# A fused group-norm, gate and 3x3-convolution kernel: the convolution moved to eight array tiles, with column folds, a channel norm on ScalarE, a new order of VectorE and POOL, and six x slots

## The chip, the cores and the metric

The kernel runs on one core of one Trainium2 chip. The metric is the device time of one execution in microseconds (us). Three runs of the kernel before took 4295.59, 4297.46 and 4298.4 us: the median is 4297.46 us. TensorE is called PE, its weight loads PEld, VectorE DVE, ScalarE ACT, GpSimd POOL, and SyncE, which issues all the DMAs, SP.

## The reference

The input x is (8, 512, 128, 128) in fp32. It is first group-normalised over 32 groups of 16 channels, and each of the 8*32 = 256 groups is then an image gx of 16 channels and 128x128 pixels:

```python
gap = mean(gx, (2, 3)); gmp = max(gx, (2, 3))
ch = conv1x1(concat([gap, gmp], 1), w_cc, b_cc)
channel_weight = sigmoid(_gn(ch, gn1_w, gn1_b))      # _gn: one element for each channel
hw = conv1x1(concat([mean over w, mean over h]), w_s1, b_s1)
pos_h = sigmoid(conv1x1(xh, w_ph, b_ph)); pos_w = sigmoid(conv1x1(xw, w_pw, b_pw))
sx = conv3x3(gx * pos_h * pos_w, w_s3) + b_s3        # 16 -> 16 channels, padding SAME
spatial_weight = sigmoid(_gn(sx, gn2_w, gn2_b))      # over the 128x128 pixels of each channel
return x + gx * (channel_weight * spatial_weight)
```

So each group needs statistics of x (mean, variance, row sums, column sums, maxima), two position gates from them, the gated image, a 3x3 convolution of it, the statistics of that, and a last multiply-add.

## The kernel before, in words

**Layout.** A unit is two groups (j = 0, 1); there are UNITS = 128. Image row 8b + r (b = 0 to 15, r = 0 to 7) of channel c lies on partition 8c + r, in band b. So a group is a tile of 128 partitions by 16 bands by 128 pixels, 2048 elements a partition. x comes into `xt` (XS = 4 slots of one unit each), in eight DMAs of 128 KB for each group, and the result leaves from `sp_buf` in eight more (L222, L230).

**Loop.** Every engine has its own `body(t, q)`, and `turns` (L165) runs it for all t. In body t PE does the convolution of unit t; DVE, ACT and POOL prepare the gates of unit a = t + 1; DVE reduces unit c = t + 2; the result of unit b = t - 1 is finished; SP loads unit t + 3 into the slot of unit t - 1, after waiting for `final` of that unit (L220). The order of instructions in each body is written by hand, with semaphores between engines.

**Convolution.** `conv(h, first, last)` (L695) handles a half group, h = 0 to 3: two PSUM banks of four bands each. A 3x3 kernel reaches the rows 8b - 1 and 8b + 8, which lie in the neighbouring bands. `W_conv` (128x128 for each kw) covers what stays in the band. For the rest SP copies the edge rows of the gated image, in three shifts, into `halo` (96 partitions, L245), and one more matmul with `W_halo` adds them. So each bank takes 3 + 1 matmuls of 512 columns, a unit 8 banks and thus 32 matmuls. Between them PE does small matmuls that sum over partitions: `mean`, `maxima`, `mean2`, `variance`, `var2`, `positions`, `channel` (all through `mm`, L637). Each fp32 matmul of the source is two instructions in the trace, each with a weight load of its own; this document calls them passes.

**VectorE.** Body t (L529 to L618) in its order: `finish(b, 0)` (two passes over the group, L524 and L527), the small `sums_n` (L543, L545), row sums of group 0 of unit c (L554), `gmx` and `var_e`, row sums of group 1, `tot`, `gate_hr` (L594), the column sums of both groups (L560, a reduction over a rearranged view), `ch` (L603), the maxima (L607), `modulate` of both groups (L567), `finish(b, 1)`.

**ACT** evicts conv_ps, 1024 elements at a time (L370), squares x (L435) and the convolution (L390) with a sum, makes the gates (L447, L452), the affine pair `scale`, `bias` (L408, L411), the sigmoid (L416) and `cgate` (L471). **POOL** makes `gate_w * gate_hr` (L323), the powers of -0.5 (L343, L275), `kfac` (L336), and the channel branch: three small operations in `channel_in` (L284 to L289) and nine in `channel_norm` (L297 to L313), each waiting for the one before.

## Time and profile of the kernel before

| what | value |
|---|---|
| median of three runs | 4297.46 us |
| the profiled execution: its own time | 4296.2 us |
| the profiled execution: span of the trace | 4294.3 us |
| PE, DVE busy, share of the span | 94%, 94% |
| ACT, POOL busy, share of the span | 61%, 41% |
| mean granted TensorE clock | 0.965 |
| HBM read and written | 268.64 MB, 268.44 MB |

The profile page gives shares of the whole span. Since the kernel is one loop of 128 equal bodies, it is read here per unit: a group's total divided by 128, and timelines of one body. Busy times of groups overlap by up to 0.1 us at their seams, so the step from one start to the next is shorter than a mean duration. Most of the time below is told as a period, the time from one unit to the next.

### The profile page before, as it was taken

What the parts mean: (1) busy time and instruction counts of PE and PEld (TensorE: products, weight loads), DVE (VectorE), ACT (ScalarE), POOL (GpSimd) and SP (SyncE); (2) the same over time, 40 slices, a digit from 0 to 9 for tenths busy, and PEclk for the clock granted to TensorE, in tenths of its full rate; (3) what the DMA queues carried; (4) which work ended last, traced back from release to release, by engine and by line L of the source; (5) the groups of instructions that cost most, each with busy time, mean ns of one, the idle gap of its engine ahead of it and who ended that gap; (6) DMA issues with size and microseconds to landing.
All of it is one profiled execution on the core that took longest, in us unless ns stands there. A gap on an engine that the chain in (4) does not pass through costs nothing.

```text
span 4294.3 us, 55492 instructions
## 1 busy us (share of the span) xinstructions
PE 4041.4 (94%) x11016; PEld 1938.2 (45%) x11016; DVE 4018.4 (94%) x2719; ACT 2624.4 (61%) x4354; POOL 1775.4 (41%) x2314
## 2 busy tenths in 40 slices
PE   5999999999999999999999999999999999999997
PEld 2444444444444444444444444444444444444443
DVE  7999999999999999999999999999999999999996
ACT  3566566666665666666656666666666666665665
POOL 3443444444434434443344434344444344434443
PEclk9999999999999999999999999999999999999998
DMA  6777777777777777777777777777777777777775
GB/s 124 163 173 173 172 175 169 175 172 173 172 173 169 177 173 172 175 167 178 172 172 172 172 176 172 171 172 176 168 177 173 172 175 167 177 173 173 171 177 123
DMA packets 1147751, 730.57 MB, mean 170 GB/s; under 512 B 74144, under 2 KB 1122976, under 8 KB 1147552
## 3 DMA queue, kind: packets, MB, share of 16 engines
q1 hardware_dynamic: 1147552, 728.87, 74.7%
q14 instruction: 190, 1.56, 0.1%
q8 instruction: 9, 0.15, 0.0%
HBM read 268.64 MB, written 268.44 MB: 125 GB/s over the span
## 4 chain that ended last, share of the span: by engine, by line
DVE 53%; issue 18%; SPq 11%; DMA 9%; PE 6%; POOL 1%; ACT 1%; DVEq 1%; POOLq 0%; ACTq 0%
DVE sums L560 13%; DVE mx L607 12%; SPq L222 11%; DMA xt<-in_x 9%; DVE sp_buf L524 7%; DVE sums L554 7%; DVE gated L567 7%; DVE sp_buf L527 6%; PE conv_ps L637 5%; POOL rstd L275 1%; ACT sp_buf L416 1%; DVE gate_hr L594 0%; PE pos_ps L637 0%; DVE ch L603 0%; DVE sums_n L545 0%
## 5 line engine op out<-in xcount | busy, mean ns | idle before, releaser
L637 PE MATMUL conv_ps<-gated,W_conv 128*128 128x512 f32 x6144 | 2973.1, 619 | 16.5 <-DVE gated L567 16.3
L637 PEld LDWEIGHTS conv_ps<-gated,W_conv 128*128 128x128 f32 x6144 | 1143.4, 197 | 1100.0 <-issue 1071.7
L637 PE MATMUL conv_ps<-halo,W_halo 96*128 96x512 f32 x2048 | 1027.7, 604 | 2.1 <-DMA halo<-gated 1.6
L370 ACT ACTIVATE sp_buf<-conv_ps,weights 128x1024 f32<-128x1024 f32 x512 | 565.3, 1104 | 747.8 <-PE conv_ps L637 747.5
L323 POOL TENSOR_TENSOR gated<-gate_w,gate_hr 128x2048 f32<-128x2048 f32 x256 | 918.7, 3609 | 166.9 <-DVE gate_hr L594 157.6
L560 DVE TENSOR_REDUCE sums<-xt 128x128 f32<-128x2048 f32 x256 | 943.6, 3725 | 0.0
L554 DVE TENSOR_REDUCE sums<-xt 128x16 f32<-128x2048 f32 x256 | 584.2, 2282 | 171.5 <-DMA xt<-in_x 171.4
L524 DVE SCALAR_TENSOR_TENSOR sp_buf<-xt,negm,sp_buf 128x2048 f32<-128x2048 f32 x256 | 600.6, 2346 | 38.3 <-ACT sp_buf L416 38.3
L527 DVE SCALAR_TENSOR_TENSOR sp_buf<-sp_buf,kfac,xt 128x2048 f32<-128x2048 f32 x256 | 602.1, 2352 | 9.0
L567 DVE SCALAR_TENSOR_TENSOR gated<-xt,negm,gated 128x2048 f32<-128x2048 f32 x256 | 593.9, 2361 | 0.0
L343 POOL TENSOR_TENSOR rstd<-var_e,consts 128x2 f32<-128x2 f32 x128 | 89.8, 701 | 1176.8 <-DVE var_e L581 1176.8
L607 DVE TENSOR_REDUCE mx<-xt 128x2 f32<-128x4096 f32 x128 | 563.7, 4404 | 0.0
L416 ACT ACTIVATE sp_buf<-sp_buf,bias,scale 128x2048 f32<-128x2048 f32 x256 | 536.4, 2095 | 8.5
L637 PEld LDWEIGHTS conv_ps<-halo,W_halo 96*128 96x128 f32 x2048 | 367.1, 190 | 379.9 <-issue 354.8
L390 ACT ACTIVATE junk<-sp_buf,negm 128x2048 bf16<-128x2048 f32 x256 | 512.5, 2002 | 41.5 <-ACT share L384 41.0
L435 ACT ACTIVATE junk<-xt,negm 128x2048 bf16<-128x2048 f32 x256 | 510.5, 1994 | 19.0 <-ACT negm L429 11.9
L275 POOL TENSOR_TENSOR rstd<-var_e,consts 128x1 f32<-128x1 f32 x256 | 234.2, 915 | 674.7 <-ACT var_e L399 674.7
L336 POOL TENSOR_TENSOR kfac<-cgate,rstd 128x2 f32<-128x2 f32 x128 | 164.8, 1288 | 390.5 <-ACT cgate L471 390.5
L447 ACT ACTIVATE gate_h<-pos_ps,b_pos,rstd 128x16 f32<-128x16 f32 x256 | 79.0, 359 | 294.6 <-POOL rstd L343 294.6
L399 ACT ACTIVATE var_e<-gn_ps,consts 128x1 f32<-128x1 f32 x256 | 68.3, 267 | 301.0 <-PE gn_ps L637 301.0
L637 PE MATMUL pos_ps<-sums_n,W_rows 128*128 128x32 f32 x256 | 57.1, 308 | 159.0 <-DVE sums_n L545 159.0
L408 ACT ACTIVATE scale<-rstd,weights 128x1 f32<-128x1 f32 x256 | 74.0, 289 | 192.5 <-POOL rstd L275 192.5
(79 smaller groups left out, 2174.4 us busy)
## 6 DMA issues: line engine op xcount, KB each, us to landing
xt<-in_x SPq DMA_DIRECT2D x2048, 128.0 KB, 3.0
out<-sp_buf SPq DMA_DIRECT2D x2048, 128.0 KB, 2.5
halo<-gated SPq DMA_DIRECT2D x512, 365.2 KB, 6.0
weights<-in_by_channel SPq DMA_DIRECT2D x1, 116.5 KB, 2.6
S_chan<-in_same_channel SPq DMA_DIRECT2D x1, 64.0 KB, 1.9
whalo_in<-in_wconv SPq DMA_DIRECT2D x2, 3.0 KB, 1.8
masks<-in_row_masks SPq DMA_DIRECT2D x1, 12.0 KB, 1.9
hmask<-in_halo_mask SPq DMA_DIRECT2D x1, 3.0 KB, 1.9
```

What stands on the lines that cost most here:

```text
L323: nc.gpsimd.tensor_tensor(gated[:, d, j, :, 1:1 + W], gate_w[:, d, j].unsqueeze(1).to_broadcast([P, NB, W]), gate_hr[:, d, j].unsqueeze(2) ...
L370: nc.scalar.activation(sp_buf[:, g, k * 8:k * 8 + 8], conv_ps[:, h % 2], ACT.Identity, bias=V["b_s3"], accum_out=ssum2[:, g, k:k + 1]).the ...
L390: nc.scalar.activation(junk[:, 2], sp_buf[:, g].rearrange("p b w -> p (b w)"), ACT.Square, bias=negm2[:, g:g + 1], accum_out=ssq2[:, g:g + ...
L416: nc.scalar.activation(flat, flat, ACT.Sigmoid, scale=scale2[:, g:g + 1], bias=bias2[:, g:g + 1]).then_inc(sig2, 1)
L435: nc.scalar.activation(junk[:, j], xt[:, sa, j].rearrange("p b w -> p (b w)"), ACT.Square, bias=negm[:, sa, j:j + 1], accum_out=ssq[:, da, ...
L524: nc.vector.scalar_tensor_tensor(flat, xf, negm[:, s, j:j + 1], flat, ALU.add, ALU.mult).then_inc(fin_a, 1)
L527: nc.vector.scalar_tensor_tensor(flat, flat, kfac[:, s, j:j + 1], xf, ALU.mult, ALU.add).then_inc(final, 1)
L554: nc.vector.tensor_reduce(sums[:, dc, j, 0:NB], xt[:, sc, j], AX_X, ALU.add).then_inc(sums_done, 1)
L560: nc.vector.tensor_reduce(sums[:, dc, j, NB:], xt[:, sc, j].rearrange("p b w -> p w b"), AX_X, ALU.add).then_inc(sums_done, 1)
L567: nc.vector.scalar_tensor_tensor(gated[:, da, j, :, 1:1 + W], xt[:, sa, j], negm[:, sa, j:j + 1], gated[:, da, j, :, 1:1 + W], ALU.add, AL ...
L607: nc.vector.tensor_reduce(mx[:, dc], xt[:, sc].rearrange("p j b w -> p j (b w)"), AX_X, ALU.max).then_inc(mx_done, 1)
L637: return nc.tensor.matmul(ps, lhsT, rhs, start=start, stop=stop)
```

## The change

x slots XS go from 4 to 6, and the loop runs six bodies a turn. Image row 8b + r of channel c now lies on partition 32*(r//2) + 2c + r%2, so that each 32 partitions hold two rows of all channels. `gated` gets an empty band at each end (18 bands), and the halo tile, its DMAs and `W_halo` go. A convolution matmul is one tile of 64 input partitions by 32 output partitions: `tiles` issues four of them (one for each pair of output rows), `slot(n)` does bank n of the unit, for each kw the four tiles of the upper 64 partitions on bank n and the four of the lower 64 partitions on bank n - 1. The row that comes from another band is reached by a band index that is one lower or higher. conv_ps is four banks, evicted two at a time as before in size. Column sums become two elementwise folds (16 bands to 8 to 4) and four accumulating matmuls; the mean is subtracted through a further matmul (`W_cols_m`, `W_rows_m`), so `sums_n` goes. `channel_in` goes into matmuls (`W_gap_m`, `W_ch_m`), `channel_norm` goes from POOL to ACT and its power joins `rstd` on POOL, as four columns.

```diff
-XS = 4
+XS = 6
...
-        gated = sb("gated", [P, 2, 2, NB, WP])
-        halo = sb("halo", [HALO, 2, 2, NB * WP])
+        gated = sb("gated", [P, 2, 2, NB + 2, WP])
...
-        conv_ps = psum("conv_ps", [P, 2, HALF * BB, W])
+        conv_ps = psum("conv_ps", [P, BANKS, BB, W])
...
+        def row_partitions(r):
+            at = QUAD * (r // 2) + r % 2
+            return slice(at, QUAD * (r // 2 + 1), 2)
...
-                v, vs = t + 3, (q + 3) % XS
-                h, hs = t + 1, (q + 1) % 2
+                v, vs = t + XS - 1, (q + XS - 1) % XS
...
                 load(0)
                 store(0)
-                halo_rows(0)
-                halo_rows(1)
                 load(1)
                 store(1)
...
# POOL
+                if real(a):
+                    pool.wait_ge(var_done, a + 1)
+                    if real(t):
+                        pool.wait_ge(ch_var, 6 * t + 6)
...
+                    nc.gpsimd.tensor_tensor(rstd[:, sa], var_e[:, sa % 2], consts[:, 0:4],
+                                            ALU.pow).then_inc(rstd_done, 1)
...
+                if real(a):
+                    gate_products(a, sa, 0)
+                if real(b):
+                    rstd2_power(b, sb_, 1)
...
+                    nc.gpsimd.tensor_tensor(kfac[:, q], cgate[:, q % 2], rstd[:, q, 0:2],
                                             ALU.mult).then_inc(kfac_done, 1)
                 if real(a):
...
                     gate_products(a, sa, 1)
-                    channel_norm(a, sa)
                 if real(t):
                     rstd2_power(t, q, 0)
...
# ACT
+            def channel_variance(u, s):
+
+                act.wait_ge(ch_mm, u + 1)
...
+                for j in range(2):
+                    nc.scalar.activation(ch[:, 0, j:j + 1], cw_ps[:, j:j + 1], ACT.Identity,
+                                         scale=rstd[:, s, j:j + 1], bias=V["b_cc"]).then_inc(ch_var, 1)
+                for j in range(2):
+                    act.wait_ge(ch_var, 6 * u + j + 1)
+                    nc.scalar.activation(ch[:, 1, j:j + 1], ch[:, 0, j:j + 1], ACT.Identity, scale=-1.0,
+                                         bias=ch[:, 0, j:j + 1]).then_inc(ch_var, 1)
+                act.wait_ge(ch_var, 6 * u + 4)
+                nc.scalar.activation(ch[:, 2], ch[:, 1], ACT.Square).then_inc(ch_var, 1)
...
+                nc.scalar.activation(var_e[:, (s + 1) % 2, 2:4], ch[:, 2], ACT.Identity,
+                                     bias=consts[:, 4:5]).then_inc(ch_var, 1)
+
+            def channel_gate(u, s):
+
+                act.wait_ge(rstd_done, u + 2)
+                for j in range(2):
+                    nc.scalar.activation(ch[:, 3, j:j + 1], ch[:, 1, j:j + 1], ACT.Copy,
+                                         scale=rstd[:, (s + 1) % XS, 2 + j:3 + j]).then_inc(ch_norm, 1)
...
+                nc.scalar.activation(cgate[:, s % 2], ch[:, 3], ACT.Sigmoid, scale=V["gn1_w"],
+                                     bias=V["gn1_b"]).then_inc(cgate_done, 1)
...
+            def body(t, q, k):
...
+                if real(a):
+                    mean1(a, sa)
+                    square1(a, sa, 0, loads(k, q, 1))
                 if real(b):
                     evacuate(b, sb_, 3)
                 if real(a):
...
+                    square1(a, sa, 1, loads(k, q, 1))
+                    gates(a, sa)
+                if real(t):
+                    evacuate(t, q, 0)
                 if real(b):
                     square2(b, sb_, 1)
                 if real(t):
...
+                    channel_gate(t, q)
+                    evacuate(t, q, 1)
                 if real(b):
                     variance2(b, sb_, 1)
...
                     spatial_gate(b, sb_, 1)
                 if real(t):
                     square2(t, q, 0)
+                    evacuate(t, q, 2)
+                if real(a):
+                    channel_variance(a, sa)
                 if real(t):
...
                     variance2(t, q, 0)
                     spatial_gate(t, q, 0)
...
# DVE
+            def fold_columns(u, s, j, come):
...
+                nc.vector.tensor_tensor(fold8[:], xt[:, s, j, 0:8], xt[:, s, j, 8:16],
+                                        ALU.add).then_inc(fold8_done, 1)
+                dve.wait_ge(fold8_done, n + 1)
...
+                nc.vector.tensor_tensor(fold4[:, s % 2, j], fold8[:, 0:4], fold8[:, 4:8],
+                                        ALU.add).then_inc(fold4_done, 1)
...
+                if real(c):
+                    fold_columns(c, sc, 0, loads(k, q, 2))
+                    fold_columns(c, sc, 1, loads(k, q, 2))
                 if real(b):
...
+                    gate_x(b, sb_, 0)
                 if real(a):
...
+                    channel_maxima(a, sa)
+                    variance1(a, sa)
+                if real(b):
+                    add_x(b, sb_, 0)
                 if real(a):
...
+                    scaled_row_gate(a, sa)
                 if real(c):
...
+                    row_sums(c, sc, 0)
+                    row_sums(c, sc, 1)
+                    totals(c, sc)
+                    maxima(c, sc)
                 if real(a):
...
+                    modulate(a, sa, 0)
+                    modulate(a, sa, 1)
                 if real(b):
...
+                    gate_x(b, sb_, 1)
+                    add_x(b, sb_, 1)
...
# PE
+                        mm(pos[:, :, 0:NB], W_rows[:, :], sums[:, da], stop=False)
+                        mm(pos[:, :, 0:NB], W_rows_m[:, :], shift.to_broadcast([P, 2, NB]), start=False)
+                        for i in range(4):
+                            mm(pos[:, :, NB:NB + W], W_cols[:, :], fold4[:, da, :, i], start=i == 0, stop=False)
+                        mm(pos[:, :, NB:NB + W], W_cols_m[:, :], shift.to_broadcast([P, 2, W]),
+                           start=False).then_inc(pos_mm, 1)
...
+                def tiles(u, d, n, half, kw, start):
+
+                    j, k = n // BANKS, n % BANKS
+                    for o in range(PAIRS):
+                        band = 1 + BB * k
+                        if half == 1 and o == 0:
+                            band -= 1
+                        if half == 0 and o == PAIRS - 1:
+                            band += 1
+                        rows = slice(ROW_TILE * half, ROW_TILE * (half + 1))
+                        cols = slice(QUAD * o, QUAD * (o + 1))
+                        ins = mm(conv_ps[cols, k], W_conv[rows, kw, cols],
+                                 gated[rows, d, j, band:band + BB, kw:kw + W], start=start and kw == 0,
+                                 stop=not start and kw == KW - 1)
+                    return ins
+
+                def slot(n, first=0, last=KW):
...
+                        if n % 2 == 0 and later(4 * t + n // 2, 2):
+                            pe.wait_ge(evac, 4 * t + n // 2 - 1)
...
+                    for kw in range(first, last):
+                        if real(t):
+                            ins = tiles(t, q % 2, n, 0, kw, True)
...
+                            if n > 0:
+                                ins = tiles(t, q % 2, n - 1, 1, kw, False)
+                            else:
+                                ins = tiles(b, sb_ % 2, 7, 1, kw, False)
...
                 mean()
-                conv(0, 0, 2)
                 maxima()
...
+                slot(0)
+                slot(1)
                 mean2(b, sb_, 1)
...
+                positions()
+                slot(2, 0, 1)
                 variance()
...
+                slot(2, 1, KW)
+                slot(3)
+                slot(4)
                 var2(b, sb_, 1)
...
                 channel()
...
+                slot(5)
                 mean2(t, q, 0)
...
+                slot(6)
+                slot(7)
                 var2(t, q, 0)
```

In the setup, `expand` writes each 128x128 weight in four instructions of 32 columns instead of one, and `gated` is cleared whole.

## Rows read from the trace of the kernel before

**Rows 1.** The profile page, engines' busy time and chain.

```profile
PE 4041.4 (94%) x11016; PEld 1938.2 (45%) x11016; DVE 4018.4 (94%) x2719; ACT 2624.4 (61%) x4354; POOL 1775.4 (41%) x2314
...
DVE 53%; issue 18%; SPq 11%; DMA 9%; PE 6%; POOL 1%; ACT 1%; DVEq 1%; POOLq 0%; ACTq 0%
```

**Rows 2.** Source view of L587: duration min/median/max, first and last start.

```profile
L587 DVE TENSOR_REDUCE tot<-sums x128: 185/186/190, 21.1 to 4194.6; 128x2 f32<-128x32 f32 x128
```

**Rows 3.** Windows: us, busy of each engine, PEclk, DMA share.

```profile
2002.11:2032.67 30.56, 30.56 (x87) 14.58 (x86) 29.31 (x22) 20.73 (x35) 13.49 (x18) 1.00 0.72 173
500.00:4200.00 3700.00, 3533.83 (x9636) 1693.38 (x9635) 3511.69 (x2354) 2293.83 (x3811) 1550.35 (x2018) 0.96 0.76 173
```

**Rows 4.** Waits view, all engines: total us, times, longest us.

```profile
ACT gate_h L447 <- POOL rstd L343: 294.6, 112, 5.8
...
DVE sums L554 <- DMA xt<-in_x: 171.4, 115, 5.7
...
DVE sp_buf L524 <- ACT sp_buf L416: 38.3, 17, 11.5
```

**Rows 5.** Chain of waits, 2028 to 2048 us: start us, us, what.

```profile
2034.96 2.36 DVE sp_buf L527
...
2037.49 0.60 SPq L222
...
2041.93 0.54 SPq L222
...
2042.65 3.25 DMA xt<-in_x
```

**Rows 6.** Timelines of PE and PEld, 2000 to 2006 us.

```profile
2002.11 0.28 PE L637 MATMUL norm_ps<-tot,M_all 128*128 128x2 f32 x2
...
2001.68 0.19 PEld L637 LDWEIGHTS norm_ps<-tot,M_all 128*128 128x128 f32 x1 [0.24 <-issue]
2002.11 0.19 PEld L637 LDWEIGHTS norm_ps<-tot,M_all 128*128 128x128 f32 x1 [0.24 <-issue]
2002.22 0.30 PEld L637 LDWEIGHTS conv_ps<-gated,W_conv 128*128 128x128 f32 x2
```

**Rows 7.** Groups by line and shape, PE: xcount, busy us, mean ns, idle before.

```profile
L637 PE MATMUL conv_ps<-gated,W_conv 128*128 128x512 f32 x6144 | 2973.1, 619 | 16.5 <-DVE gated L567 16.3
...
L637 PE MATMUL conv_ps<-halo,W_halo 96*128 96x512 f32 x2048 | 1027.7, 604 | 2.1 <-DMA halo<-gated 1.6
```

**Rows 8.** Timeline of DVE, one body.

```profile
2004.65 2.35 DVE L524 SCALAR_TENSOR_TENSOR sp_buf<-xt,negm,sp_buf 128x2048 f32<-128x2048 f32 x1
...
2009.30 0.23 DVE L543 TENSOR_SCALAR sums_n<-sums,negm 128x16 f32<-128x16 f32 x1
...
2009.97 2.28 DVE L554 TENSOR_REDUCE sums<-xt 128x16 f32<-128x2048 f32 x1
...
2016.13 7.39 DVE L560 TENSOR_REDUCE sums<-xt 128x128 f32<-128x2048 f32 x2
...
2023.51 4.40 DVE L607 TENSOR_REDUCE mx<-xt 128x2 f32<-128x4096 f32 x1
...
2037.23 2.34 DVE L524 SCALAR_TENSOR_TENSOR sp_buf<-xt,negm,sp_buf 128x2048 f32<-128x2048 f32 x1
```

**Rows 9.** Groups by line and shape, DVE.

```profile
L524 DVE SCALAR_TENSOR_TENSOR sp_buf<-xt,negm,sp_buf 128x2048 f32<-128x2048 f32 x256 | 600.6, 2346 | 38.3 <-ACT sp_buf L416 38.3
...
L488 DVE TENSOR_TENSOR w_part<-weights,masks 128x128 f32<-128x128 f32 x6 | 1.8, 292 | 0.2
```

**Rows 10.** Groups by line and shape, ACT and POOL.

```profile
L411 ACT ACTIVATE bias<-negm,weights,scale 128x1 f32<-128x1 f32 x256 | 99.1, 387 | 8.5
...
L307 POOL TENSOR_TENSOR ch<-ch,consts 128x2 f32<-128x2 f32 x128 | 89.8, 702 | 10.0
...
L408 ACT ACTIVATE scale<-rstd,weights 128x1 f32<-128x1 f32 x256 | 74.0, 289 | 192.5 <-POOL rstd L275 192.5
...
L303 POOL TENSOR_TENSOR ch<-ch 128x2 f32<-128x2 f32 x128 | 27.0, 211 | 10.0
```

More of the change, by code:

```diff
@@ L73, in conv_attention @@
         S_chan = sb("S_chan", [P, P])
-        sums = sb("sums", [P, 2, 2, NB + W])
-        sums_n = sb("sums_n", [P, 2, 2, NB + W])
+        sums = sb("sums", [P, 2, 2, NB])
+        fold8 = sb("fold8", [P, 8, W])
+        fold4 = sb("fold4", [P, 2, 2, 4, W])
+        W_rows_m = sb("W_rows_m", [P, P])
+        W_cols_m = sb("W_cols_m", [P, P])
         tot = sb("tot", [P, 2, 2])
@@ L167, in turns, with loads @@
             first, last = 1, (UNITS - 4) // PER
-            for t in range(-3, first * PER):
-                body(t, t % PER)
+            for t in range(1 - XS, first * PER):
+                body(t, t % PER, t // PER)
             with eng.Fori(first, last) as turn:
                 for q in range(PER):
-                    body(turn * PER + q, q)
+                    body(turn * PER + q, q, turn)
             for t in range(last * PER, UNITS + 1):
-                body(t, t % PER)
+                body(t, t % PER, t // PER)
+        def loads(k, q, d):
+            return 16 * RB * (k + (q + d) // XS + 1)
         ends = [0]
@@ L417, in spatial_gate, with mean1, square1 @@
                                      bias=bias2[:, g:g + 1]).then_inc(sig2, 1)
-            def body(t, q):
+            def mean1(u, s):
+                act.wait_ge(mean_mm, u + 1)
+                if later(u, XS):
+                    act.wait_ge(final, 2 * (u - XS) + 2)
+                nc.scalar.activation(negm[:, s], norm_ps[:, 0:2], ACT.Copy, scale=-1.0).then_inc(negm_done, 1)
+            def square1(u, s, j, come):
+                if j == 0:
+                    act.wait_ge(negm_done, u + 1)
+                act.wait_ge(x_in[s][j], come)
+                if later(u, 1):
+                    act.wait_ge(sq_done, 2 * u + j - 1)
+                nc.scalar.activation(junk[:, j], xt[:, s, j].rearrange("p b w -> p (b w)"), ACT.Square,
+                                     bias=negm[:, s, j:j + 1], accum_out=ssq[:, s % 2, j:j + 1]).then_inc(sq_done, 1)
@@ L525, in finish, with add_x @@
+            def add_x(u, s, j):
+                g = 2 * (s % 2) + j
+                n = 2 * u + j
+                flat = sp_buf[:, g].rearrange("p b w -> p (b w)")
                 dve.wait_ge(fin_a, n + 1)
                 dve.wait_ge(kfac_done, u + 1)
-                nc.vector.scalar_tensor_tensor(flat, flat, kfac[:, s, j:j + 1], xf, ALU.mult, ALU.add).then_inc(final, 1)
-            def body(t, q):
+                nc.vector.scalar_tensor_tensor(flat, flat, kfac[:, s, j:j + 1],
+                                               xt[:, s, j].rearrange("p b w -> p (b w)"),
+                                               ALU.mult, ALU.add).then_inc(final, 1)
@@ new lines, in scaled_row_gate, with modulate @@
+            def scaled_row_gate(u, s):
+                dve.wait_ge(gates_done, 4 * u + 4)
+                dve.wait_ge(rstd_done, u + 1)
+                if later(u, 2):
+                    dve.wait_ge(gp_done, 2 * (u - 1))
+                nc.vector.tensor_tensor(gate_hr[:, s % 2], gate_h[:, s % 2],
+                                        rstd[:, s, 0:2].unsqueeze(2).to_broadcast([P, 2, NB]),
+                                        ALU.mult).then_inc(ghr_done, 1)
+            def modulate(u, s, j):
+                dve.wait_ge(gp_done, 2 * u + j + 1)
+                inner = gated[:, s % 2, j, 1:1 + NB, 1:1 + W]
+                nc.vector.scalar_tensor_tensor(inner, xt[:, s, j], negm[:, s, j:j + 1], inner,
+                                               ALU.add, ALU.mult).then_inc(mod_done, 1)
@@ L615, in body @@
-                modulate(0)
-                modulate(1)
+                    modulate(a, sa, 0)
+                    modulate(a, sa, 1)
                 if real(b):
-                    finish(b, sb_, 1)
+                    gate_x(b, sb_, 1)
+                    add_x(b, sb_, 1)
             turns(dve, body)
```

437 lines of the change are left out of this document (159 added, 278 removed).

## The prediction, made before the changed kernel was run

> **What bounds the kernel now.** I read the engines' busy shares first. DVE and PE both stand at 94% [rows 1], so one engine's share decides nothing. Then the rhythm: `tot` starts once a unit, first at 21.1 and last at 4194.6 us [rows 2], which makes a period of 4173.5/127 = 32.86 us. The rest of the execution (4296.2 us by its own time) is 123 us of start and end. I make the sum against that execution; it stands 1.3 us below the median of the runs, which I neglect.
>
> PE is not the bound: between two `mean` matmuls with no stall it does a whole unit in 30.56 us [rows 3], 2.3 us less than the period. The chain is 53% DVE, 18% issue gaps, 11% SP's queue, 9% DMA and 6% PE [rows 1], and in one body it shows the loop: DVE ends `final`, SP issues the eight loads into the freed slot (the first at 2037.49, the seventh at 2041.93, so 0.74 us each), the last lands 3.25 us after its issue, and only then do the row sums start [rows 5]. DVE waits for x 171.4 us in all [rows 4], 1.34 us a unit. So DVE's own work is 32.86 - 1.34 = 31.5 us a unit, with 38.3/128 = 0.3 us of waiting for ACT in it [rows 4].
>
> **VectorE.** Out go the four `sums_n` (2009.30 to 2009.97, 0.67 us) and both column sums with `ch` (2016.13 to 2023.51, 7.38 us) [rows 8]: 8.05 us. In come, for each group, an elementwise add of 1024 elements and one of 512. No such add of these lengths is in the trace. An elementwise add of 128 took 0.292 us and a two-tensor pass over 2048 took 2.346 [rows 9]; a straight line between them gives 1.25 and 0.70 us. The bounds for a unit's folds: 1.15 ns an element (2346/2048) and nothing fixed gives 3.5 us; the column sums' own 3.69 us for 2048, spent on 1536, gives 5.5. I take the line, 3.9 us, because the pass it leans on is the same kind of work. DVE then needs 31.5 - 8.05 + 3.9 = 27.4 us (27.0 to 29.0). Splitting `finish` in two moves work and adds none; between `gate_x` and `add_x` now stand two tiny operations, which cover the latency of the first.
>
> **x slots.** A load of unit t+5 still waits for `final` of unit t-1, but DVE needs it three bodies later instead of one. The whole SP and DMA piece of the chain, about 1.34 us, is thus covered by two bodies. It is already out of my 27.4. SP still issues 32 DMAs, 32*0.74 = 23.7 us, and loses the four halo ones; it fits under 27 but not far under: the next thing late there would be the stores, on which evictions wait. DMA was busy 0.76 of the time with the halo traffic [rows 3] and loses that part.
>
> **TensorE, convolution.** A pass of 512 columns steps by 0.43 us (weight loads at 2001.68 and 2002.11 [rows 6]), at a granted clock of 1.00 in this stretch and 0.96 in the loop as a whole [rows 3], that is at the 2.4 GHz level nearly all the time. Now 64 passes, 27.5 us, leaving 30.56 - 27.5 = 3.0 us for the small matmuls. After: 8 slots x 3 kw x 8 tiles = 192 matmuls, 384 passes. If the eight tiles stream at once this is 24 full matmuls: 48*0.43 = 20.6 us, or 54 ns a pass. That is the lower bound; with no overlap, the upper bound, it is 384*0.43 = 165 us. The trace has no tile, so what speaks for one end? Issue: between two weight loads of a small matmul lie 0.11 us (2002.11, 2002.22 [rows 6]) for 128 columns; a tile loads 32, a quarter, 28 ns, under the 54. So loads need not hold the tiles up, and the halves of the array differ in rows, columns and banks. I take 20.6.
>
> The TensorE page of the Trainium skill (TensorE: Matmul & The Clock Gate, "Measured speedup vs the span model") gives 10.6x for 16 tiles and 2.38x for 3 column tiles, with one pass a tile. No run here shows it.
>
> **TensorE, the rest.** `positions` gains four matmuls of 256 columns (2*0.215 = 0.43 us each, half of 512): 1.7 us. `W_rows_m` and one channel matmul are load-bound, 2*0.11 us each: 0.4. Then the changes between whole-array and tile matmuls: five stretches of small matmuls a unit, ten changes. If each waits for the matmul in flight to leave the array, it costs what a matmul lasts beyond its step, 604 [rows 7] - 430 = 174 ns: 1.7 us. The bounds are nothing and a whole matmul, 6 us. I take 1.7, as the array must be emptied but not idle longer. Sum: 20.6 + 3.0 + 1.7 + 0.4 + 1.7 = 27.5 us (25.8 to 31.8).
>
> The Trainium skill (TensorEngine Tiling (Array Packing), "Key Properties") says that changing the tiling mode drains the engine. Without it the sum would be 25.8 and DVE alone the bound.
>
> **ACT and POOL.** ACT works 2624.4/128 = 20.5 us [rows 1] and gains eight one-or-two-element operations, at 0.29 to 0.39 us [rows 10]: 2.6. It waits 294.6/128 = 2.3 us for `rstd` [rows 4]. 23.1 + 2.3 = 25.4 us: under the others, though its evictions are due sooner. A bank pair came free again after a half of 6.9 us; now one slot, 2.6 us, lies between its last write and its next, and ACT's squares and sigmoids are 2 us long. POOL loses nine and three small operations (0.70, and 0.2 each [rows 10]), about 2.9 of 13.9 us. But `gate_products(a, 1)` now stands behind `rstd2_power(b, 1)` and `kfac`, which wait for ACT; DVE's 9 us of row sums and maxima (2*2.28 + 4.40 [rows 8]) cover that; without it `modulate` would be late.
>
> **The sum.** DVE 27.4 and PE 27.5 us are level, and each waits for the other once or twice a unit. For the seams I add 0.6 us, twice what DVE waits for ACT now: 28.1 us a unit. The setup has 45 more small linked DVE instructions, under 0.29 us each [rows 9], and clears all of `gated` (9360 elements, at most 10.7 us at 1.15 ns); the first shortened units give part of this back: +7. So 127*28.1 + 123 + 7 = 3699, say **3700 us**.
>
> **The rivals.**
> First, *the tiles do not run side by side*. Each tile gets two passes in a row. If a matmul may start only after the one before it in the program, the second pass of a tile holds the queue until the first has streamed, and each tile matmul costs 0.43 us: 192*0.43 = 82.6, plus 6.9 = 89.5 us a unit, 11,500 us. For it: the two passes in sequence, each with its own load [rows 6]. Against it: nothing in this trace. The point of decision is 67.6 ns a pass ((32.86 - 6.9)/384); above it the kernel is slower. The TensorE page of the Trainium skill ("The mechanism") says that matmuls start and end strictly in program order, which would give just this. A milder form, the tiles packed at two thirds: 31.2 + 6.9 = 38.1 us, 4970 us. Chance of both: 0.18, two thirds of it for the first.
>
> Second, *PE or ACT is the bound, still faster*. At 60 ns a pass and 0.4 us a change PE needs 23.0 + 5.1 + 4 = 32.1 us: 4210 us. Or each of four evictions comes 0.5 us late for its bank and PE stands: 27.5 + 2 = 29.5 us, 3880 us. ACT's order is strict and it has 3 us to spare. 0.30.
>
> Third, *DVE alone*: no change cost, full cover: 26.8 to 27.4 us, 3530 to 3610 us. 0.10.
>
> Fourth, *no gain*: the tile passes land between 66 and 69 ns by chance. 0.02.
>
> **How the numbers follow.** My forecast, 27.5 to 29.0 us a unit (3620 to 3810 us), has 0.40. Adding the third and nearly all of the second, 3520 to 4230 us holds about 8 in 10. Faster by over 0.2% (about what a measurement of this kernel can tell from no change): 0.40 + 0.30 + 0.10 = 0.80; within: 0.02; slower: 0.18.
>
> **What would show it.** Column adds at 1.25 and 0.70 us on DVE; no wait of row sums or folds for x; tile passes stepping by about 54 ns, eight in flight; a stop of 0.17 us where small matmuls follow tiles; a step of `tot` of 28.1 us; ACT at 82% busy. The forecast falls if the tile passes step by more than 60 ns, or if PE's waits for evictions pass 1 us a unit.

## The result, and the profile after

The changed kernel takes 4532.26 us (median of four runs, 4530.24 to 4536.99) against 4296.52 us before: 1.0551 times the time before (95% interval 1.0533 to 1.057). The forecast was 3700 us. The page of the changed kernel:

```profile
span 4528.4 us, 140298 instructions
PE 3905.6 (86%) x53512; PEld 1885.3 (42%) x53512; DVE 3564.3 (79%) x2380; ACT 2889.1 (64%) x5378; POOL 1706.1 (38%) x777
```

Every engine has less to do than in [rows 1] or has room left, and none is full. The beat comes from the source view of `tot` (duration, first and last start):

```profile
L560 DVE TENSOR_REDUCE tot<-sums x128: 185/186/188, 42.2 to 4436.4; 128x2 f32<-128x32 f32 x128
```

(4436.4 - 42.2)/127 = 34.60 us a unit, where [rows 2] gave 32.86. What stands outside the 127 periods is 4532 - 4394 = 138 us; I had 123 + 7.

TensorE in one body (start us, us, then in brackets the idle time before and what ended it):

```profile
2007.90 0.38 PE L653 MATMUL gn_ps<-ssq,M_chan 128*128 128x1 f32 x2
...
2008.67 5.74 PE L653 MATMUL conv_ps<-gated,W_conv 64*32 64x512 f32 x96
2017.62 0.38 PE L653 MATMUL gn_ps<-ssum,M_chan 128*128 128x2 f32 x2 [3.20 <-ACT sp_buf L322]
...
2018.41 3.62 PE L653 MATMUL pos_ps<-fold,W_cols 128*128 128x256 f32 x8
...
2022.39 1.09 PE L653 MATMUL conv_ps<-gated,W_conv 64*32 64x512 f32 x16
2023.41 0.38 PE L653 MATMUL norm_ps<-ssq,M_all 128*128 128x2 f32 x2
2023.73 4.88 PE L653 MATMUL conv_ps<-gated,W_conv 64*32 64x512 f32 x80
2029.79 3.11 PE L653 MATMUL conv_ps<-gated,W_conv 64*32 64x512 f32 x48 [1.18 <-ACT sp_buf L322]
...
2042.54 0.38 PE L653 MATMUL gn_ps<-ssq,M_chan 128*128 128x1 f32 x2
```

Three things are to be seen. Two slots of convolution, as much work as twelve passes over the whole array (12*0.43 = 5.16 us), take 5.74 us, so the tiles do run side by side. PE stands twice for an eviction (L322 is `evacuate`), 3.20 us ahead of `mean2(b, 1)` and 1.18 us ahead of slot 4. And the eight fold passes, 256 columns each, take 3.62 us where eight halves of 0.43 us should take 1.7. The windows view of the same stretches says why (us; busy us of PE, PEld, DVE, ACT, POOL; granted clock; DMA share; GB/s):

```profile
2008.67:2014.40 5.73, 5.73 (x97) 2.39 (x96) 5.69 (x3) 2.85 (x5) 2.58 (x1) 1.00 0.01 3
...
2017.62:2022.00 4.38, 4.38 (x15) 3.73 (x16) 1.96 (x2) 1.93 (x2) 0.00 (x0) 0.61 0.66 171
```

Before the stand the clock is 1.00 (2.4 GHz); after it, most of the positions run at 1.2 GHz. Over the whole span the mean granted clock is 0.938, and 0.965 before. As the clock has two levels, one half the other, a mean m means 2(1 - m) of the span at the low one: 561 us now, 301 us before.

The timelines of ACT, POOL and DVE around these waits, one fence for each:

```profile
2011.36 0.29 ACT L360 ACTIVATE scale<-rstd,weights 128x1 f32<-128x1 f32 x1 [2.78 <-POOL rstd L260]
...
2012.11 2.10 ACT L368 ACTIVATE sp_buf<-sp_buf,bias,scale 128x2048 f32<-128x2048 f32 x1
...
2014.38 2.00 ACT L385 ACTIVATE junk<-xt,negm 128x2048 bf16<-128x2048 f32 x1
...
2016.38 1.09 ACT L322 ACTIVATE sp_buf<-conv_ps,weights 128x1024 f32<-128x1024 f32 x1
...
2027.23 0.62 ACT L395 ACTIVATE gate_h<-pos_ps,b_pos,rstd 128x16 f32<-128x16 f32 x2 [7.68 <-POOL rstd L285]
...
2028.43 1.12 ACT L322 ACTIVATE sp_buf<-conv_ps,weights 128x1024 f32<-128x1024 f32 x1
```

```profile
2008.75 2.58 POOL L260 TENSOR_TENSOR rstd<-var_e,consts 128x1 f32<-128x1 f32 x1 [4.63 <-ACT var_e L351]
2024.26 2.88 POOL L285 TENSOR_TENSOR rstd<-var_e,consts 128x4 f32<-128x4 f32 x1 [12.93 <-DVE var_e L589]
```

```profile
2023.84 0.16 DVE L589 TENSOR_SCALAR var_e<-norm_ps 128x2 f32<-128x2 f32 x1 [4.25 <-PE norm_ps L653]
```

Read in order of time these rows are one ring through all the engines. `var2(t, 0)` on PE at 2007.90; ACT's `var_e` and POOL's power, 2.58 us long; ACT's spatial gate from 2011.36, then, by the new order, `mean1`, the first square, and only then the eviction of (b, 3), ended 2017.57; PE's `mean2(b, 1)`, positions and variance, to 2023.8; DVE's `var_e`; POOL's power of four, 2.88 us; ACT's gates and then the eviction (t, 0); PE's slot 4 at 2029.79, after which PE runs without a gap to the next `var2(t, 0)` at 2042.54. From link to link: 0.85 + 2.61 + 6.26 (ACT) + 6.22 (PE) + 0.42 + 2.97 + 2.56 + 12.75 = 34.64 us, the period. The totals of the waits view (us, times, longest):

```profile
ACT gate_h L395 <- POOL rstd L285: 996.6, 127, 16.8
...
DVE var_e L589 <- PE norm_ps L653: 577.2, 128, 7.3
ACT scale L360 <- POOL rstd L260: 443.4, 256, 2.8
...
PE gn_ps L653 <- ACT sp_buf L322: 346.5, 109, 3.3
...
PE conv_ps L653 <- ACT sp_buf L322: 135.5, 114, 1.2
```

The wait for x of [rows 4] is gone. The stand ahead of `mean2(b, 1)` comes in 109 of the 128 units. Once a turn of the loop, 18 times in all, PE stands instead at its first instruction with nothing to wait for (`PE norm_ps L653 <- issue`, 49.7 us in all, up to 3.1 us a time); the kernel before has no such wait.

### The profile page after: what moved, and what is told of

Its sections match the earlier page's. It is cut to its first block and busy times, and to the rows that moved or that the text cites. A ratio compares the mean times of both kernels' runs of the same rounds, so it can differ in the third digit from the quotient of the medians.

```text
span 4528.4 us, 140298 instructions
## 1 busy us (share of the span) xinstructions
PE 3905.6 (86%) x53512; PEld 1885.3 (42%) x53512; DVE 3564.3 (79%) x2380; ACT 2889.1 (64%) x5378; POOL 1706.1 (38%) x777
## 3 DMA queue, kind: packets, MB, share of 16 engines
q14 instruction: 241, 1.97, 0.1%
## 5 line engine op out<-in xcount | busy, mean ns | idle before, releaser
L653 PE MATMUL conv_ps<-gated,W_conv 64*32 64x512 f32 x49152 | 3031.2, 600 | 150.9 <-ACT sp_buf L322 135.5
L653 PEld LDWEIGHTS conv_ps<-gated,W_conv 64*32 64x32 f32 x49152 | 1118.2, 107 | 1539.8 <-issue 1440.1
L285 POOL TENSOR_TENSOR rstd<-var_e,consts 128x4 f32<-128x4 f32 x128 | 368.4, 2878 | 1726.2 <-DVE var_e L589 1726.2
L395 ACT ACTIVATE gate_h<-pos_ps,b_pos,rstd 128x16 f32<-128x16 f32 x256 | 80.4, 360 | 996.7 <-POOL rstd L285 996.6
L260 POOL TENSOR_TENSOR rstd<-var_e,consts 128x1 f32<-128x1 f32 x256 | 395.2, 1544 | 836.6 <-ACT var_e L351 836.6
L322 ACT ACTIVATE sp_buf<-conv_ps,weights 128x1024 f32<-128x1024 f32 x512 | 566.7, 1107 | 11.6 <-PE conv_ps L653 9.2
L589 DVE TENSOR_SCALAR var_e<-norm_ps 128x2 f32<-128x2 f32 x128 | 20.4, 159 | 577.2 <-PE norm_ps L653 577.2
L653 PE MATMUL pos_ps<-fold,W_cols 128*128 128x256 f32 x1024 | 410.9, 572 | 0.0
L653 PE MATMUL gn_ps<-ssum,M_chan 128*128 128x2 f32 x512 | 101.7, 268 | 346.5 <-ACT sp_buf L322 346.5
L541 DVE TENSOR_TENSOR fold<-xt 128x1024 f32<-128x1024 f32 x256 | 312.8, 1222 | 16.1 <-DVE fold L546 5.0
L653 PEld LDWEIGHTS gn_ps<-ssum,M_chan 128*128 128x128 f32 x512 | 79.7, 196 | 568.8 <-ACT sp_buf L322 442.1
L653 PEld LDWEIGHTS pos_ps<-fold,W_cols 128*128 128x128 f32 x1024 | 284.7, 291 | 55.7
```

The costliest lines, as they stand in the source:

```text
L260: nc.gpsimd.tensor_tensor(rstd2[:, g:g + 1], var2_e[:, g:g + 1], consts[:, 0:1], ALU.pow).then_inc(rstd2_done, 1)
L322: nc.scalar.activation(sp_buf[:, g, 8 * k:8 * k + 8], conv_ps[:, 2 * k:2 * k + 2], ACT.Identity, bias=V["b_s3"], accum_out=ssum2[:, g, k:k ...
L653: return nc.tensor.matmul(ps, lhsT, rhs, start=start, stop=stop)
```

## The experiments

My theory after the result was this ring: the order of in-order queues sets the period, and the low clock after PE's long stand adds to it. The rivals: the clock is only a symptom; the powers on POOL, held up by DVE, are the cause; the late variance is; the six slots or the pace of the tiles matter more. Every edit below is against the changed kernel unless it says otherwise, and the ratio is always to the kernel before. "To stand" is said of an engine that is idle because it waits. "Period" is worked out from `tot` as above.

**e3_evac3: the eviction goes back ahead of the squares.**

```diff
+                if real(b):
+                    evacuate(b, sb_, 3)
                 if real(a):
                     mean1(a, sa)
                     square1(a, sa, 0, loads(k, q, 1))
-                if real(b):
-                    evacuate(b, sb_, 3)
-                if real(a):
                     square1(a, sa, 1, loads(k, q, 1))
```

> ACT evicts the last half of unit b ahead of mean and the first square of unit a, instead of behind them. The half has been ready 2 us and more when ACT comes to it, and PE stands 3.2 us before mean2 for it. Ring theory: that wait falls to about 1.0 us, the period by 2.0, the time to 4270 to 4330 us. Rival T: PE's wait moves elsewhere and the time stays within 0.5% of 4532 us.

Measured: 4094.63 us, 0.9533 (0.9517 to 0.9549), period 31.18 us, mean clock 0.989. TensorE's timeline, and the window of its positions:

```profile
2016.45 0.39 PE L652 MATMUL gn_ps<-ssum,M_chan 128*128 128x2 f32 x2 [0.94 <-ACT sp_buf L322]
...
2017.21 1.97 PE L652 MATMUL pos_ps<-fold,W_cols 128*128 128x256 f32 x8
...
2027.09 3.02 PE L652 MATMUL conv_ps<-gated,W_conv 64*32 64x512 f32 x48 [1.18 <-ACT sp_buf L322]
```

```profile
2016.45:2019.55 3.10, 3.10 (x17) 2.56 (x17) 3.06 (x3) 2.99 (x4) 0.00 (x0) 1.00 0.60 176
```

The stand shrinks by 3.20 - 0.94 = 2.26 us and the fold passes, now at full clock, by 3.62 - 1.97 = 1.65 us. Together 3.9 us, and a usual body is now 30.74 us (one `mean2` group at 2003.02 us, the same one of the next unit at 2033.76), where the one shown above had 34.64. The place of one eviction in ACT's queue is the whole difference between slower and faster than before. Its wait alone doesn't explain the gain; the clock is two fifths of it, and that part I hadn't priced: I expected 4270 us at best.

**e6_fill: PE is given more to do.** This kernel adds work: four matmuls of 384 columns, whose result nothing reads, ahead of `mean2(b, 1)`.

```diff
 slot(1)
+if real(a):
+    if later(a, 1):
+        pe.wait_ge(gates_done, 4 * a)
+    for i in range(4):
+        mm(pos_ps[:, 0:KW * P], W_cols[:, :], W_conv[:].rearrange("p k n -> p (k n)"))
 mean2(b, sb_, 1)
```

> The changed kernel, with four matmuls of 384 columns ahead of mean2(b, 1) whose result is overwritten unread: 2.6 us of work put into PE's wait of 3.2 us for the eviction, where nothing is computed that is used. Theory C (PE's wait drops the granted clock to its lower level for 3.4 or 6.8 us after it, and positions and a part of the convolution then run at half pace): the granted clock rises from 0.938 to 0.98 or more, the eight fold passes take 2.0 us instead of 3.6, and the time FALLS by 1 to 2 us a unit, to 4270 to 4400 us, though PE has more to do. Rival R (the ring of waits alone sets the time and the clock follows it): the time stays within 0.5% of 4532 us or rises.

Measured: 4414.53 us, 1.0271 (1.0252 to 1.0289), period 33.72 us, mean clock 0.982.

```profile
2006.43 2.85 PE L653 MATMUL pos_ps<-W_conv,W_cols 128*128 128x384 f32 x8
2009.71 0.38 PE L653 MATMUL gn_ps<-ssum,M_chan 128*128 128x2 f32 x2 [0.43 <-ACT sp_buf L322]
...
2010.46 1.97 PE L653 MATMUL pos_ps<-fold,W_cols 128*128 128x256 f32 x8
```

With the eviction as late as in the changed kernel, and more work on PE, the kernel is 118 us faster. Nothing in the ring was relieved but the fold passes, 3.62 to 1.97 us. So the clock is a cause and no symptom, and it is worth 0.9 us of the mean period and up to 1.65 us of a single one. The clock rose and the fold passes shortened as I expected; the time ended 15 us above my range.

**e1_addx: POOL's power of four is freed from DVE's two-input pass.** DVE does `add_x(b, 0)` earlier and a row sum in its old place.

```diff
                 if real(b):
                     gate_x(b, sb_, 0)
+                    add_x(b, sb_, 0)
                 if real(a):
                     channel_maxima(a, sa)
                     variance1(a, sa)
-                if real(b):
-                    add_x(b, sb_, 0)
+                if real(c):
+                    row_sums(c, sc, 0)
                 if real(a):
                     scaled_row_gate(a, sa)
                 if real(c):
-                    row_sums(c, sc, 0)
                     row_sums(c, sc, 1)
```

> DVE's add_x of group 0 moves ahead of the variance step, and a row sum (one input tensor) stands behind it instead. In the changed kernel the power of four columns on POOL took 2.88 us beside add_x (two input tensors), the power of two columns of the kernel before 0.70 us beside a row sum. Theory L (POOL's small operations are held while DVE runs a two-input operation, and this lies on a ring of waits through all engines): the four-column power falls under 1.0 us, and the period of 34.60 us falls by up to 2.0, the time to 4280 to 4350 us. Rival P (four columns of power cost 2.9 us by themselves): it stays at 2.9 us and the time within 0.5% of 4532 us. Rival T (the tile convolution itself sets the time): the power may fall, the time stays.

Measured: 4445.38 us, 1.0349 (1.0332 to 1.0366), period 33.90 us, mean clock 0.899. The groups of POOL and DVE that changed (xcount, busy us, mean ns, idle before):

```profile
L285 POOL TENSOR_TENSOR rstd<-var_e,consts 128x4 f32<-128x4 f32 x128 | 129.6, 1012 | 1845.1 <-DVE var_e L589 1845.1
```

```profile
L571 DVE TENSOR_TENSOR maxima_in<-mx,mask_pix 128x16 f32<-128x16 f32 x128 | 423.3, 3307 | 4.4
```

The power falls from 2878 to 1012 ns: beside a row sum, which has one input, it isn't held. PE's 1.18 us wait at slot 4 goes. But the hold turns round: `maxima_in`, 176 ns in the kernel before and 900 in the changed one, now starts beside POOL's gate product and takes 3.3 us, for which almost no engine waits here (8.2 us in all). Of the 1.87 us saved in the ring 0.70 came out. The timeline shows the rest:

```profile
2014.39 0.59 PE L653 MATMUL gn_ps<-ssum,M_chan 128*128 128x2 f32 x2 [3.21 <-ACT sp_buf L322]
...
2015.69 3.76 PE L653 MATMUL pos_ps<-fold,W_cols 128*128 128x256 f32 x8
...
2020.23 1.27 PE L653 MATMUL conv_ps<-gated,W_conv 64*32 64x512 f32 x16
```

From `mean2` to slot 2 it is now 5.84 us, where the changed kernel has 4.77, and the conv passes after it lose 0.18 more: 1.2 us given back to the clock. 1.87 - 1.25 = 0.6, against 0.70 measured. The stand of 3.21 us is untouched, and the low clock lasts longer behind it. So the theory was right on the power, and the 4280 to 4350 us that I drew from it were too low.

**e2_pevar: the variance comes between the fold passes.**

```diff
 mm(pos[:, :, NB:NB + W], W_cols[:, :], fold4[:, da, :, i], start=i == 0, stop=False)
+if i == 1:
+    variance()
...
-slot(2, 0, 1)
-variance()
-slot(2, 1, KW)
+slot(2)
```

> PE issues the variance matmul after the second of the four fold matmuls instead of after positions and a third of slot 2, where it came 3.9 us after the squares were done. Ring theory: rstd comes 3 to 4 us earlier, ACT's gates and the eviction behind them too; that takes away PE's wait for that eviction (1.18 us in the body read) but not the 3.2 us before mean2, so the period falls by 1 to 1.5 us, to about 33.4, 4370 to 4400 us. Rival T (PE's own work sets the time): within 0.5% of 4532 us.

Measured: 4436.48 us, 1.0328 (1.0311 to 1.0345), period 33.85 us, mean clock 0.900. ACT's wait for the power of four falls from 996.6 to 628.6 us, 2.9 us a unit, and slot 4 no longer waits; but the period falls by 0.75 us only, less than the 1 to 1.5 us that I expected, and again the low level takes more: 2(1 - 0.900) of 4435 us, 887 us. The stand is 3.21 us here too, and the eight fold passes, 1.97 us at full clock, take 2.05 + 2.06 us. e1 and e2 cut different links of the ring and end at the same time; both leave the stand and the clock behind it, and I take these for the reason.

**e4_xs4: four x slots instead of six.**

```diff
-XS = 6
+XS = 4
```

> Four x slots instead of six, the loop back to four bodies a turn. VectorE now has 7 us of slack in each body, so the loads have more time. Ring theory: no DMA on the ring, the time within 0.5% of 4532 us. Rival D (the slots are what keeps x on time): VectorE waits for x again, more than 1 us a unit, and the time rises above 4600 us.

Measured: 4910.88 us, 1.1433 (1.1414 to 1.1452), period 37.52 us.

```profile
DVE fold L541 <- DMA xt<-in_x: 831.3, 124, 7.7
```

The rival that the slots matter was right: the column folds stand early in DVE's body, and with four slots they wait 6.5 us a unit for x. The two more slots are worth 2.9 us a unit here and not the 1.34 us at which I put the old wait. The clock is in this figure too: at a mean of 0.908 the low level takes 902 us instead of 561, which costs up to half the difference, 1.3 us a unit.

**e8_e3addx: e3 and e1 together.**

```diff
+                    evacuate(b, sb_, 3)
...
-                    evacuate(b, sb_, 3)
...
                     gate_x(b, sb_, 0)
+                    add_x(b, sb_, 0)
```

> Eviction first on ACT (4095 us by itself) and add_x ahead of the variance step on DVE (4445 us by itself). If the two-input hold of POOL is a cost of its own, the four-column power is 1.0 us again instead of 2.9, ACT's gates and the eviction behind them come 1.9 us sooner and PE's wait of 1.18 us before slot 4 goes: period 29.5 to 30.0, time 3900 to 3980 us. If PE's own work sets the time already: within 1% of 4095 us.

Measured: 4071.44 us, 0.9474 (0.9457 to 0.9491), period 31.00 us, mean clock 0.981. With the stand mended, freeing the power brings 23 us and not the 115 or more that I expected. ACT's wait for the power of four is still 486.7 us (526.9 in e3), and the hold has moved to DVE: `maxima_in` takes 3.08 us (0.90 in e3), which brings DVE to 94% of the span, 30.0 of the 31.0 us of a period.

**e5_all3: e3, e1 and e2 together.**

```diff
+                    evacuate(b, sb_, 3)
...
+                    add_x(b, sb_, 0)
...
+                            if i == 1:
+                                variance()
```

> All three: eviction first, add_x ahead, variance among the fold matmuls. Then no wait of the ring is left that I know, and PE's own work is the bound: 28.9 us a unit at the full clock (30.74 less waits of 0.94 and 1.18, and a seam), 3820 to 3900 us. If more waits come up that I do not see: above 3920 us.

Measured: 4185.85 us, 0.974 (0.9714 to 0.9766), period 31.88 us, mean clock 0.947. Slower than e8 by 114 us: two new waits.

```profile
DVE gated L604 <- POOL gated L271: 437.1, 107, 7.6
...
PE norm_ps L652 <- ACT junk L385: 192.8, 126, 2.5
```

```profile
2004.33 3.61 POOL L271 TENSOR_TENSOR gated<-gate_w,gate_hr 128x2048 f32<-128x2048 f32 x1 [2.00 <-DVE gate_hr L596]
2012.08 1.62 POOL L260 TENSOR_TENSOR rstd<-var_e,consts 128x1 f32<-128x1 f32 x1 [4.14 <-ACT var_e L351]
...
2013.82 3.61 POOL L271 TENSOR_TENSOR gated<-gate_w,gate_hr 128x2048 f32<-128x2048 f32 x1
```

The second gate product stands behind `rstd2_power(b, 1)`, which waits 4.14 us for ACT; now that the gates come early nothing on DVE covers that. And the variance in the middle of the folds asks for ACT's second square some 1.5 us (192.8/126) before it is there. Where PE stood 2.30 and 2.38 us for it, the four fold passes behind took 2.06 us, at low clock; where it stood 1.08 to 1.50 us they took 1.11, at full clock. Over the run the low level takes 444 us, where e8 has 155.

**e7_lag: the lower tiles a round further behind the upper ones (on e5).**

```diff
-if real(t) if n > 0 else real(b):
-    if kw == 0:
+m, low = (n - 1, kw - 1) if kw > 0 else (n - 2, KW - 1)
+if real(t) if m >= 0 else real(b):
+    if low == 0:
         pe.wait_ge(upper_mm, 8 * t + n)
```

> All three, and the tiles of the lower 64 partitions follow the upper ones by four rounds instead of three, so that PE does not stand at each slot's start until the last upper tile has left the array. Two slots took 5.74 us to the last end, 5.58 to the last step, against 12 rounds of 0.43 = 5.16 us. Theory: 0.2 us a slot comes back, 1.7 us a unit; PE needs about 27.2, VectorE about 27.4: period 27.4 to 28.2, time 3600 to 3720 us. Rival (the 0.2 us is something else, such as the change of bank): the time stays that of the run with all three.

Measured: 4513.41 us, 1.0503 (1.0485 to 1.0522), period 34.39 us, mean clock 0.906.

```profile
2026.45 5.39 PE L652 MATMUL conv_ps<-gated,W_conv 64*32 64x512 f32 x96
```

Two slots take 5.39 instead of 5.74 us: the lower tiles' wait for `upper_mm` at the start of slot 7, which follows slot 6 directly, had cost 0.35 us. Slots 1 and 3 also follow another directly; three times 0.35 is 1.05 us a unit. It is paid for elsewhere. A bank is finished a round later; ACT's evictions wait for PE 790.6 us (337.3 in e5) and DVE for the gate product 734.8 us. PE in turn stands 482.7 us for ACT's `junk` (its squares of x) and `var_e`, where e5 has 247.9, and the low level takes 848 us instead of 444, which costs up to half the difference, 202 us. The engine got faster, the ring longer and the clock lower.

**e10_gp: both gate products ahead of `rstd2_power(b, 1)` (on e8).**

```diff
                 if real(a):
                     gate_products(a, sa, 0)
+                    gate_products(a, sa, 1)
                 if real(b):
                     rstd2_power(b, sb_, 1)
...
-                if real(a):
-                    gate_products(a, sa, 1)
                 if real(t):
                     rstd2_power(t, q, 0)
```

> Eviction first and add_x ahead, as in the run of both (4071 us), and POOL makes both gate products one after the other, ahead of rstd2_power(b, 1) and kfac. In that run the hold worked the other way too: DVE's maxima_in, a two-input operation of 16 elements, took 3.14 us (0.18 us in the kernel before) beside the second gate product, and DVE worked without a gap. Theory L (POOL and DVE exclude each other in two-input operations): maxima_in falls under 1.2 us, the period from 30.72 to 29.0 to 30.0, time 3850 to 3980 us. Rival: rstd2_power(b, 1), now 2 us later, holds up the sigmoid and the finish; the time stays within 1% of 4071 us.

Measured: 4055.98 us, 0.9443 (0.9427 to 0.9459), period 30.78 us, mean clock 0.951. It changes little, 15 us, as the rival had it, but not for the rival's reason: DVE's wait for the sigmoid is 27.8 us in all (22.3 in e8). `maxima_in` falls from 3.08 to 0.66 us and `kfac` rises from 0.20 to 1.86: the hold moves on to whoever comes next. What was freed on DVE went to a new stand of PE, 134.2 us in 107 units, and to the clock behind it:

```profile
2015.61 0.40 PE L651 MATMUL cw_ps<-maxima_in,M_chan 128*128 128x16 f32 x2 [1.33 <-ACT var_e L419]
2015.94 7.44 PE L651 MATMUL conv_ps<-gated,W_conv 64*32 64x512 f32 x96
```

Two slots take 7.44 us here instead of 5.74, at a granted clock of 0.77. Over the run the low level takes 396 us, where e8 has 155; up to half the difference, 121 us, is lost by it. So a stand of 1.33 us can be followed by the low level too.

**e9_all4: the products together (on e5).**

```diff
                     gate_products(a, sa, 0)
+                    gate_products(a, sa, 1)
...
-                if real(a):
-                    gate_products(a, sa, 1)
```

> The run with all three edits (4186 us), in which DVE waited 437 us for the second gate product, and the products one after the other. Theory: that wait goes, 3.4 us a unit, PE (28.6 us of its own) is next: 3880 to 3980 us. Rival (the early variance matmul, for which PE stands 1.4 us a unit waiting for ACT's squares, is what made the three slower than the two): above 4050 us.

Measured: 4259.54 us, 0.9912 (0.9896 to 0.9929), period 32.53 us, mean clock 0.938. DVE's wait for the product is gone, and the kernel is 74 us slower than e5: the rival here was right too. PE still stands 182.0 us for ACT's squares, now 113.4 us for `var_e` (55.1 in e5), and DVE waits 258.3 us for ACT's spatial gate (24.3 in e5), whose power stands behind both products.

**e11_var3: the variance after the last of the four fold matmuls (on e10, which has it in slot 2; e9 has it after the second).**

```diff
+    if i == 3:
+        variance()
...
-slot(2, 0, 1)
-variance()
-slot(2, 1, KW)
+slot(2)
```

> As the run before this one, with the variance matmul after the fourth fold matmul instead of the second, where ACT's squares are done and PE does not stand. Theory: rstd about 1.4 us sooner than with it in slot 2, no new wait: 3800 to 3930 us, the fastest so far. Rival: another wait comes up, time within 1% of the run with the two edits and the products together.

Measured: **3875.98 us, 0.9031 (0.9015 to 0.9046)**, period 29.44 us, mean clock 0.986. This is the best version found and beats both kernels.

```profile
PE 3628.8 (94%) x53512; PEld 1720.1 (44%) x53512; DVE 3549.7 (92%) x2380; ACT 2898.6 (75%) x5378; POOL 1491.1 (38%) x777
```

```profile
1999.83 0.38 PE L651 MATMUL norm_ps<-ssq,M_all 128*128 128x2 f32 x2 [0.95 <-ACT junk L384]
```

It differs from e9 in the place of the variance, two fold matmuls later. That is 384 us, 3.09 us a unit. PE's waits for ACT fall from (182.0 + 113.4)/128 = 2.3 to (96.1 + 18.2)/128 = 0.9 us, and the time at the low level from 529 to 108 us, of which half, 1.65 us a unit, is lost at most. Those two make 3.05 us. Against e10, which differs in this edit alone, it is 180 us: PE's stand for `var_e` goes from 134.2 to 18.2 us and the low level from 396 to 108 us, and the stand for the squares, 96.1 us, is new.

**e12_lag4: the lag of e7 on the best version.**

```diff
+m, low = (n - 1, kw - 1) if kw > 0 else (n - 2, KW - 1)
+if real(t) if m >= 0 else real(b):
+    if low == 0:
```

> As the last, and the lower tiles four rounds behind the upper ones. With the lag two slots took 4.8+0.6 = 5.39 us instead of 5.74 in the run that had it, but each half is evicted 0.9 us later. Theory (PE's own work is the bound): PE needs 1.4 us less a unit and the time falls by 100 to 180 us against the last run. Rival (the ring of waits is the bound): a later eviction lengthens it by up to 0.9 us a crossing and the time rises, as 4513 us against 4186 us did.

Measured: 4376.54 us, 1.0189 (1.017 to 1.0209), period 33.35 us, mean clock 0.921. Evictions wait for PE 726.3 us against 277.4 in e11. As in e7, the pace of PE is bought with lateness at the eviction, and here too the clock is a large part: the low level takes 691 us against 108, which costs up to 291 of the 501 us lost.

## Why the prediction was wrong

**What held.** The prices of single operations did. The folds take 1.222 and 0.692 us (forecast 1.25 and 0.70), in these groups:

```profile
L541 DVE TENSOR_TENSOR fold<-xt 128x1024 f32<-128x1024 f32 x256 | 312.8, 1222 | 16.1 <-DVE fold L546 5.0
L546 DVE TENSOR_TENSOR fold<-fold 128x512 f32<-128x512 f32 x256 | 177.1, 692 | 10.4
```

The wait for x is gone; DVE works 27.8 us a unit (27.4). ACT's new small operations take 0.20 to 0.39 us. The tiles stream eight abreast, 54 ns a pass, as PE's weight loads show:

```profile
2000.07 0.15 PEld L653 LDWEIGHTS conv_ps<-gated,W_conv 64*32 64x32 f32 x8 [0.28 <-issue]
2000.49 0.15 PEld L653 LDWEIGHTS conv_ps<-gated,W_conv 64*32 64x32 f32 x8 [0.28 <-issue]
2000.93 0.15 PEld L653 LDWEIGHTS conv_ps<-gated,W_conv 64*32 64x32 f32 x8 [0.28 <-issue]
```

Eight loads in 0.15 us, the next eight 0.42 to 0.44 us later.

**What was mis-sized.** PE's own work at full clock is 28.6 us: the usual body of e3 is 30.74 us, less 0.94 and 1.18. I had 27.5. The missing term is the wait of the lower tiles for the upper ones' last matmul, 1.05 us (e7). With the ten changes of tiling at the 0.12 us found below instead of 0.17, the sum comes to 28.0 us, and 0.6 us stays unexplained. A second missing term is the turn of the loop, 49.7/128 = 0.4 us a unit. So PE and not DVE would have been the bound, by 0.8 us. POOL's powers I took over at the durations of before; I left out that DVE's two-input passes hold them, 2.9 us for 1.0. Two slips changed nothing: the 0.292 us row that I called an add is a product with a mask, and tiles packed at two thirds cost 31.0 us and not 31.2.

**The step that failed** is "For the seams I add 0.6 us, twice what DVE waits for ACT now", and under it ACT "under the others, though its evictions are due sooner". I compared sums of busy time and took the largest. No engine's sum decides in the changed kernel; the ring does, 34.6 us. I had each of its links on the page and didn't join them: I wrote that only one slot now lies between a bank's last write and its next and that ACT's squares are 2 us long, and I costed the new order of ACT's queue, in which the eviction stands behind a square and the first `mean1`, at nothing. e3 prices that one move at 4532 - 4095 = 438 us. The prediction's own condition, that it falls if PE's waits for evictions pass 1 us a unit, came true: (346.5 + 135.5)/128 = 3.8 us.

**The clock** had no term at all. The prediction noted 0.96 for the loop before and took it as given. In the units read, each stand of 3.2 us was followed by fold passes that took 3.3 to 3.7 us instead of 1.97. e6 shows it with the least doubt.

**The rivals.** That the tiles do not run side by side, the only slower case I had, is refuted by the loads above. The Trainium skill (TensorE: Matmul & The Clock Gate, "The mechanism") says that matmuls start and end in program order; the rounds of eight don't speak against that, but my reading, that a tile's second pass then blocks the queue for a whole stream, was wrong. The second rival, evictions that come late, had the right mechanism: two are late, by 3.2 and 1.2 us, where I took four by 0.5. It ended at 3880 us because it let the wait fall on PE alone, without what the late positions do to DVE, POOL and ACT, and so back to PE. The cover I named for the second gate product (9 us of row sums and maxima) was good in the changed kernel, where DVE waited for it 7.9 us in all; e5 shows what it costs once the cover is gone.

**What stays open.** The low time isn't split into cause and effect in e5, e7, e9, e10 and e12: in each of them PE's stands and the low level rise together. Nor do the runs say how long a stand may be: 1.33 us in e10 was followed by the low level, 1.50 us in e5 was not. A lag of the tiles with more banks, so that the eviction isn't later, wasn't tried. The best version still has PE standing 0.75 us a unit for ACT's squares, and some 3 us at each of the eighteen turns of the loop (52.4 us in all). In the turn read, the two slots behind that stand took 7.43 us instead of 5.74. What holds PE at the turn wasn't tested.

## What to carry to other kernels

When a change shortens the two busiest engines and reorders in-order queues, follow one buffer round all the engines, with every instruction that stands ahead of it in each queue, and add up that ring before believing the largest busy sum. Put evictions that free a bank ahead of long work that nobody waits for, and give a matmul that needs a late operand its place by when that operand is ready: here two matmuls' distance was 9% of the time. Price a stand of TensorE of 3 us, and in doubt one of 1.3 us, at more than itself, for what follows it may run at half clock; read the mean granted clock of every variant beside its time, and expect a saving elsewhere to be given back while such a stand remains.

## What the hardware showed that I had not expected

- **DVE and POOL hold each other for nearly a whole instruction.** POOL's power on 128x4 takes 1.01 us beside a one-input row sum and 2.88 beside a two-input pass of 2.35 us; its power on 128x1 0.54 and 2.58; DVE's 128x16 product 0.18 us alone and, in e1, mostly 3.38 (at most 3.48) beside POOL's 3.61 us gate product. The Trainium skill (SBUF — State Buffer, "Who interferes with whom") says that a VectorE instruction with two SBUF inputs contends with a GpSimd instruction that reads SBUF, that the ports they share are an exclusive lock, and that the order of issue decides who is blocked. The traces agree, in both directions: in each pair above, the later one ends only after the earlier has ended. I should have drawn on it.
- **More work made the kernel faster**, 118 us of 4532, by keeping TensorE at 2.4 GHz (e6).
- **Changing the tiling** costs 0.12 us a time, where I had 0.17. One slot and the `mean2` group behind it take 3.05 us to the next slot, of which 2.58 are the slot's six rounds and 0.22 the group's two passes; 0.25 us are left for two changes:

```profile
2033.82 2.81 PE L653 MATMUL conv_ps<-gated,W_conv 64*32 64x512 f32 x48
2036.55 0.38 PE L653 MATMUL gn_ps<-ssum,M_chan 128*128 128x2 f32 x2
2036.87 5.74 PE L653 MATMUL conv_ps<-gated,W_conv 64*32 64x512 f32 x96
```
